# Four spill and four gather transfers per chunk in place of one and sixteen, and first-layer products done early in chunk 0

## What is computed

```python
dots = jnp.einsum('bfd,bgd->bfg', bottom_output, bottom_output)
pairs = dots[:, _TRIL_I, _TRIL_J]                     # 351 numbers per sample
x = jnp.concatenate([bottom_mlp_output, pairs, pad], axis=1)   # 480 wide
for w, b in ((w0, b0), (w1, b1), (w2, b2), (w3, b3)):  # 1024, 1024, 512, 256
    x = jax.nn.relu(x @ w.T + b)
return x @ w_out.T + b_out
```

## Time and profile before

| | us |
|---|---|
| median of 3 runs | 575.12 (574.05 to 575.9) |
| the profiled execution's own time | 574.64 |
| its span, first to last instruction | 572.8 |
| PE busy with matmuls | 90% of the span |
| ACT busy | 58% |
| POOL busy | 46% |
| DMA engines busy with SP's queue | 46% |

### The profile page before, as it was taken

How to read it: one execution, slowest core, us unless ns; L and a number is a source line. 1 busy time by engine, 2 the same in 40 slices (tenths; PEclk the granted TensorE clock), 3 DMA queues, 4 the chain that set the end, 5 groups by cost and what they waited for, 6 DMA issues and landing times.

```text
span 572.8 us, 13768 instructions
## 1 busy us (share of the span) xinstructions
PE 515.9 (90%) x4073; PEld 506.0 (88%) x4073; DVE 280.3 (49%) x646; ACT 334.4 (58%) x844; POOL 262.5 (46%) x467
## 2 busy tenths in 40 slices
PE   6948977999999699969999699979999699979997
PEld 6938976999999699969999699969999699979996
DVE  2845875527751477326761377316761377412111
ACT  3635799527982389525992389625993289613112
POOL 2801266224773177513773167613774167623321
PEclk9987999899999799998999799998999799997999
DMA  9978572255722576127732577117732477110000
GB/s 243 281 259 197 135 117 46 79 92 79 112 35 78 85 119 109 62 40 121 116 50 75 84 116 114 62 32 122 117 57 74 77 126 110 46 41 1 1 1 1
DMA packets 263088, 53.16 MB, mean 93 GB/s; under 512 B 248950, under 2 KB 260246, under 8 KB 263062
## 3 DMA queue, kind: packets, MB, share of 16 engines
q1 hardware_dynamic: 262374, 52.66, 46.0%
q10 hardware_dynamic: 688, 0.16, 0.1%
HBM read 45.71 MB, written 7.09 MB: 92 GB/s over the span
## 4 chain that ended last, share of the span: by engine, by line
PE 66%; SPq 11%; DMA 8%; ACT 4%; issue 4%; POOL 3%; DVE 2%; ACTq 1%; POOLq 0%
PE acc L684 52%; SPq L378 11%; PE gram_ps L647 8%; DMA blocks<-grams 5%; ACT parts L775 3%; PE gram_ps L630 3%; DMA pairs<-blocks 2%; PE gram_ps L601 2%; ACT h_full L791 1%; PE turned_ps L606 1%; ACTq L378 1%; POOL parts L526 1%; POOL grams L533 1%; DMA early_rows<-in_r_bottom_output_dram 1%; DVE grams L888 1%
## 5 line engine op out<-in xcount | busy, mean ns | idle before, releaser
L684 PE MATMUL acc<-h_a,w_hi 128*128 128x256 f32 x1152 | 216.0, 286 | 1.4 <-POOL h_a L541 1.2
L684 PEld LDWEIGHTS acc<-h_a,w_hi 128*128 128x128 f32 x1152 | 180.2, 193 | 3.3 <-POOL h_a L541 2.8
L791 ACT ACTIVATE h_full<-acc,small_t 128x256 f32<-128x256 f32 x176 | 82.6, 473 | 148.7 <-PE acc L684 146.2
L541 POOL TENSOR_TENSOR h_a<-h_full,h_a 128x256 fp32r<-128x256 f32 x96 | 72.3, 753 | 204.0 <-DVE h_a L908 204.0
L684 PE MATMUL acc<-h_a,w_lo 128*128 128x256 f32 x576 | 163.2, 283 | 0.0
L775 ACT ACTIVATE parts<-gram_ps 27x216 f32<-27x216 f32 x448 | 152.4, 340 | 16.0 <-PE gram_ps L647 6.5
L684 PE MATMUL acc<-x,w_hi 128*128 128x256 f32 x512 | 109.9, 313 | 34.3 <-ACT h_full L791 25.8
L684 PEld LDWEIGHTS acc<-x,w_hi 128*128 128x128 f32 x512 | 91.3, 219 | 36.1 <-issue 22.8
L684 PEld LDWEIGHTS acc<-h_a,w_lo 128*128 128x128 f32 x576 | 110.8, 192 | 0.0
L684 PE MATMUL acc<-h_b,w_hi 128*128 128x256 f32 x512 | 94.2, 285 | 2.4 <-POOL h_b L541 2.4
L908 DVE CAST h_a<-h_full 128x256 fp32r<-128x256 f32 x96 | 29.2, 304 | 123.3 <-ACT h_full L791 123.3
(11 more groups left out here) (49 smaller groups left out, 390.0 us busy)
## 6 DMA issues: line engine op xcount, KB each, us to landing
rows<-in_r_bottom_output_dram SPq DMA_DIRECT2D x444, 64.0 KB, 2.0
blocks<-grams SPq DMA_DIRECT2D x8, 864.0 KB, 3.5
w_raw<-in_L_rec_w_dram SPq DMA_DIRECT2D x6, 1024.0 KB, 7.5
early_rows<-in_r_bottom_output_dram SPq DMA_DIRECT2D x12, 224.0 KB, 6.0
stage_pairs<-in_L_rec_w_dram SPq DMA_DIRECT2D x1, 1408.0 KB, 9.5
w_raw<-in_L_rec_w_dram SPq DMA_DIRECT2D x2, 512.0 KB, 8.9
mlp_rows<-r_bottom_mlp_output_dram SPq DMA_DIRECT2D x8, 128.0 KB, 2.2
pairs<-blocks SPq DMA_DIRECT2D x32, 31.5 KB
```

What stands on the lines that cost most here:

```text
L541: nc.gpsimd.tensor_tensor(h[:, m, 1, :], h_full[:, slot % 2, :], h[:, m, 0, :].bitcast(F32), ALU.subtract).then_inc(split_done, 1)
L684: last = nc.tensor.matmul(acc_slot(slot), weight(wp, layer, m, k), in_tile(layer, k, xp), start=(k == 0 and n == 0), stop=(k == K_TILES[la ...
L791: nc.scalar.activation(h_full[:, slot % 2, :], acc_slot(slot), ACT.Relu, bias=small_t[:, slot:slot + 1]).then_inc(drained, 1)
```

## The change

`blocks` gets a new shape: for each of the 32 by 27 pairs of features now lie all 256 samples of the chunk together, 1 KB, the four quads' 64 behind one another.

- A gather piece is one transfer with runs of 1 KB; a chunk takes four gather transfers.
- A spill is four transfers, one for each quad (`spill_quad`). A quad's partition still reads its 6,912 bytes in one row, but they go to 27 places in DRAM, 256 bytes in each.
- In chunk 0, SP spills quads 0 and 1 and ACT quads 2 and 3. ACT does so before its copy of the bottom network's tile and of the weight groups.
- SP loads units 0 to 3 of chunk c+2 before the spill of chunk c+1, not after its gather.
- In chunk 0 the products of row tile 0 (k = 0) of the output tiles m = 0 to 5 come first, ahead of every product with pairs (`EARLY_TILES`). Tiles 2 and 3 are summed in the banks of `turned_ps`, tiles 4 and 5 in two banks of `gram_ps`. The weight groups 9 to 24 then have two banks, where they had four: PE waits at group n until DVE is done with group n - 2. The hooks still fire after every six matmuls, so groups 9, 10 and 11 are turned among the early products.

```diff
@@ -64,7 +64,7 @@
 EARLY_BY_ACT = 1
-OUT_HOOK = 2
+OUT_HOOK, EARLY_TILES = 2, 6
@@ -140,7 +140,7 @@
             steps.append(("early", u - XT_LAG))
-    steps.append(("mlp",))
+    steps += [("spill",), ("mlp",)]
     for n in range(BEFORE_CHUNK):
@@ -172,24 +172,30 @@
+    def products(layer, m, k, k1):
+        nonlocal done
+        while k < k1:
+            n = k1 - k
+            if layer < 2:
+                n = min(n, (every - done % every) // 3)
+            steps.append(("mm", layer, m, k, k + n))
+            k += n
+            done += 3 * n
+            if layer < 2 and done % every == 0 and hooks:
+                steps.extend(hooks.pop())
+            if done == OUT_HOOK * every:
+                steps.append(("out",))
+    if first:
+        for m in range(EARLY_TILES):
+            products(0, m, 0, 1)
     for layer in range(3):
...
                 steps.append(("mlp",))
-            k = 0
-            while k < K_TILES[layer]:
-                n = K_TILES[layer] - k
-                if layer < 2:
-                    n = min(n, (every - done % every) // 3)
-                steps.append(("mm", layer, m, k, k + n))
-                k += n
-                done += 3 * n
-                if layer < 2 and done % every == 0 and hooks:
-                    steps.extend(hooks.pop())
-                if done == OUT_HOOK * every:
-                    steps.append(("out",))
+            products(layer, m, 1 if first and layer == 0 and m < EARLY_TILES else 0, K_TILES[layer])
     if gram:
@@ -301,7 +307,7 @@
         y_view = y.rearrange("(c n) o -> c o n", n=CHUNK)
-        blocks = nc.dram_tensor("blocks", (GROUP, QUAD, FEATS, RUN), F32).ap()
+        blocks = nc.dram_tensor("blocks", (QUAD, FEATS, CHUNK), F32).ap()
@@ -311,7 +317,10 @@
-        def acc_slot(slot):
+        def acc_slot(c, slot):
+            if isinstance(c, int) and c == 0 and 2 <= slot < EARLY_TILES:
+                return (turned_ps if slot < 4 else gram_ps)[:, slot - 2, 0:CHUNK]
             return acc[:, slot % ACC_RING, 0:CHUNK]
@@ -328,7 +337,8 @@
-            return gram_ps[:, n % (GRAM_RING * GRAM_BANKS), :]
+            among = EARLY_TILES // 3 if BEFORE_CHUNK <= n < LATE_WEIGHTS else GRAM_RING * GRAM_BANKS
+            return gram_ps[:, n % among, :]
@@ -370,12 +380,14 @@
+        def spill_quad(engine, s):
+            engine.dma_start(blocks[:, :, s * RUN:(s + 1) * RUN], grams[QUAD * s:QUAD * (s + 1)]).then_inc(spilled, 16)
         def gather_piece(engine, f, nf, nk, q):
-            for s in range(GROUP):
-                src = bass.AP(blocks.tensor, (s * QUAD * FEATS + (FEATS + 1) * f + 1) * RUN,
-                              [[(FEATS + 1) * RUN, nf], [RUN, nk], [1, RUN]])
-                engine.dma_start(pairs[q % P:q % P + nf * nk, q // P, s * RUN:(s + 1) * RUN], src).then_inc(gathered[q // P], 16)
+            src = bass.AP(blocks.tensor, ((FEATS + 1) * f + 1) * CHUNK, [[(FEATS + 1) * CHUNK, nf], [CHUNK, nk], [1, CHUNK]])
+            engine.dma_start(pairs[q % P:q % P + nf * nk, q // P], src).then_inc(gathered[q // P], 16)
@@ -429,16 +441,17 @@
-            def spill(d):
+            def spill(d, quads=range(GROUP)):
...
                     sp.wait_ge(early_moved, UNITS)
-                sp.dma_start(blocks.rearrange("s f g r -> (s f) (g r)"), grams[:, :, :].rearrange("p g r -> p (g r)")).then_inc(spilled, 16)
+                for s in quads:
+                    spill_quad(sp, s)
             def gather(d, pieces=PIECES):
-                sp.wait_ge(spilled, (d + 1) * 16)
+                sp.wait_ge(spilled, (d + 1) * GROUP * 16)
                 if isinstance(d, int) and d == 0:
@@ -459,11 +472,11 @@
                         store_y(c - 1)
-                spill(c + 1)
-                gather(c + 1)
                 if not (isinstance(c, int) and c == CHUNKS - 2):
...
                         load_rows(c + 2, u)
+                spill(c + 1)
+                gather(c + 1)
@@ -483,7 +496,7 @@
                 load_weights(1, w1, 2 * i, 2 * i + 2, w1_loaded[i])
-            spill(0)
+            spill(0, (0, 1))
             load_weights(1, w1, 6, 8, w1_loaded[3])
@@ -529,7 +542,7 @@
-                    pool.wait_ge(spilled, d * 16)
+                    pool.wait_ge(spilled, d * GROUP * 16)
                 nc.gpsimd.tensor_tensor(
@@ -566,6 +579,9 @@
                     pe.wait_ge(grams_done, UNITS)
+                elif BEFORE_CHUNK <= n < LATE_WEIGHTS:
+                    pe.wait_ge(w_done, max(n - 1, BEFORE_CHUNK))
                 elif ring <= n < LATE_WEIGHTS:
@@ -666,10 +682,11 @@
-                        pe.wait_ge(w_done, groups_for(layer, m))
-                    if not (isinstance(c, int) and c == 0 and slot < ACC_RING):
-                        pe.wait_ge(drained, slot_count(c, slot) - ACC_RING)
+                        pe.wait_ge(w_done, W0_GROUPS if layer == 0 and m >= 4 else groups_for(layer, m))
+                    if not (isinstance(c, int) and c == 0 and slot < EARLY_TILES):
+                        of = slot - EARLY_TILES if isinstance(c, int) and c == 0 and slot < M_TILES[0] else slot - ACC_RING
+                        pe.wait_ge(drained, slot_count(c, of))
                 for k in range(k0, k1):
@@ -681,7 +698,7 @@
                     for n, (wp, xp) in enumerate(((w_hi, 0), (w_hi, 1), (w_lo, 0))):
-                        last = nc.tensor.matmul(acc_slot(slot), weight(wp, layer, m, k), in_tile(layer, k, xp),
+                        last = nc.tensor.matmul(acc_slot(c, slot), weight(wp, layer, m, k), in_tile(layer, k, xp),
                                                 start=(k == 0 and n == 0), stop=(k == K_TILES[layer] - 1 and n == 2))
@@ -788,7 +805,7 @@
                     act.wait_ge(weighed, 2 * c - 1 + slot)
-                nc.scalar.activation(h_full[:, slot % 2, :], acc_slot(slot), ACT.Relu,
+                nc.scalar.activation(h_full[:, slot % 2, :], acc_slot(c, slot), ACT.Relu,
                                      bias=small_t[:, slot:slot + 1]).then_inc(drained, 1)
@@ -797,7 +814,7 @@
                 for t in range(3):
-                    act.wait_ge(gathered[t], (d + 1) * 16 * GROUP * PIECES_OF[t])
+                    act.wait_ge(gathered[t], (d + 1) * 16 * PIECES_OF[t])
                     nc.scalar.activation(x0[:, 1 + t, 0, :], pairs[:, t, :], ACT.Copy).then_inc(pairs_hi_done, 1)
@@ -833,8 +850,13 @@
                     early_move(step[1])
+                elif step[0] == "spill":
+                    act.wait_ge(grams_done, UNITS)
+                    act.wait_ge(early_moved, UNITS)
+                    for s in (2, 3):
+                        spill_quad(nc.scalar, s)
                 elif step[0] == "gather":
-                    act.wait_ge(spilled, 16)
+                    act.wait_ge(spilled, GROUP * 16)
                     act.wait_ge(pairs_zeroed, 1)
```

## The result

The changed kernel takes 534.5 us (532.18 to 538.76, 4 runs); the kernel before took 574.89 in the same session. The ratio is 0.9305, with a 95% interval from 0.9243 to 0.9367: 7% faster, 40.4 us. I had said 533, with a range from 528 to 549. A second session gave 533.4 us and a ratio of 0.9293 (0.9262 to 0.9325).

The account below looks back on a forecast made before the run. The prediction took late pairs, held by one queue's 16 gather issues, to bound the kernel; the 572.8 us span less 38.2 (boundaries, last chunk's start) and 3.5 (chunk 0), plus 1.84 outside, gave 533 us, range 528 to 549.

Parts of the forecast that it names:

- The bound: Ends of chunks: PE's drain wait is ACT's wait for pairs; 11.8 of 17.0 us are one queue's issue time.
- Gather: Each boundary: four issues replace 16, so the gather takes 4.9 us, bounds 4.5 and 6.5.
- Spill: Each boundary: writing 3,456 pieces of 256 B takes 5.4 us, bounds 3.5 and 9.5.
- The disputed price: Spill: writing a 256 B piece costs the gather's 19 ns, 4.1 us in all; the skill's read-modify-write rule suggested double.
- the latency: Spill: 1.3 of the old spill's 3.5 us were not engine time, and were kept for the new spill.
- first rival: Spill: short writes cost double, spill 9.5 us, pairs 2.0 late; 548 us, 560 with the low clock; chance 0.18.
- Sum and slack: Boundaries: spill plus gather 10.3 us against a 12.4 us deadline, 2.1 to spare; chunks 58.6 us apart, saving 38.2.
- signs that I had set for being wrong: Profile: ACT still waiting for pairs at chunk ends, spill over 7.5 us, or PE gaps at chunk 0's weight groups.
- third rival: Spill: quad writes crawl; break-even 12.1 us, 50 ns a piece; at 65 ns, 600 us; chance 0.04.
- Chunk 0: Start: spill landed 38.1, tile 1 at 41.5, PE at weight group 11 at 44.5; gain 3.5 us, bounds 0 and 6.
- two banks in place of four: Chunk 0's weight groups: costs nothing; otherwise each of 14 groups would give back a few tenths.
- Reordered row loads: SP's queue: sixteen loads ahead of the spill, 8.5 us of issue, fit in its 13 us waits for the last sums.

Follow-up runs that it names:

- gather_16_issues: Changed kernel with each gather transfer cut back into four of 256 B runs, 16 issues a chunk: 595.18 us, ratio 1.0372.
- spill_written_twice: Changed kernel, but from chunk 1 on each quad's sums are also written to a second scratch, and the gather waits for all eight transfers: 571.22 us, ratio 0.9952.
- split_behind_groups: Changed kernel with ACT's and DVE's splits of chunk 0's pairs moved behind weight groups 9 to 11: 533.98 us, ratio 0.9303.
- chunk0_all_three: Changed kernel with chunk 0's pair splits behind weight groups 9-11, fourth w1 load behind SP's gather, ACT's gather issues behind group 7 and biases: 532.82 us.
- early_only: Kernel before with only the early products and two banks added; old spill, sixteen gather transfers and SP order: 573.78 us, ratio 1.0006.
- rows_behind_gather: Changed kernel with the sixteen row loads back behind the gather instead of ahead of the spill: 533.86 us, ratio 0.929.
- spill_two_queues: Changed kernel with ACT issuing quads 2 and 3 of every spill and SP quads 0 and 1: 535.38 us, ratio 0.9324.

## Why the prediction was right, point by point

**The bound.** PE's wait for a drain was a wait for pairs, and the pairs waited for issues. `gather_16_issues` shows it: with 16 issues the gap is there again, and larger.

**Gather, 4.9 us forecast.** 5.4 us measured (241.55 to 246.95). Four issues took 3.06 us, 0.77 each where I had 0.74, and from the last issue's start, 2.3 us in, to the landing there were 3.1 us instead of 2.65. My figure was a little too low, and the measured one lies inside the bounds of 4.5 and 6.5.

**Spill, 5.4 us forecast.** 6.68 measured, inside the bounds of 3.5 and 9.5. The disputed price was right: 19.4 ns a piece against the 19 that I took, and 4.3 us for a whole further copy against 4.1. The term that was too small is the latency, the 1.3 us left over by the old single transfer. With four transfers it is 2.35, of which 0.3 to 0.4 go away with a second queue. An issue took 0.86 us, not 0.53, though that too lies mostly beside the data. That the first rival's price didn't come can be said of the piece itself: writing 256 B takes the engine time of reading it, and 128 B take 12.2 ns where the row loads of that length had 13. The Trainium skill, "DMA: Bandwidth & Descriptors" (Specifications), has a read-modify-write below 512 B; no doubling of a piece shows in these rows.

**Sum and slack.** 10.3 us forecast, 12.1 measured; the deadline of 12.4 us was 12.5. Of 2.1 us to spare 0.43 were left. The forecast of 58.6 us a chunk held exactly, because the error of 1.8 us stayed below the slack, not because it was small. One of the signs that I had set for being wrong, that ACT still waits for pairs at the ends of chunks, is there in the letter: 0.48 us at the end of chunk 1. It comes from these two terms and reached PE nowhere. Three splits in one go, as I had it, are found at the end of chunk 0 only. The boundaries and the last chunk's start gave 38.4 us against 38.2.

**The first rival.** Its mechanism was refuted, and its size as well. I priced 4.1 us more on the spill at 548 us, or 560 with the clock, and 4 us of each were for chunk 0. `spill_written_twice` has 4.3 more, none of it in chunk 0, and takes 571: the lateness counts from a slack of 0.43 and not of 2.1 us, and the low clock does come behind each gap. So the boundaries cost 37 us where I had 11, or 24 with the clock. Had the pieces cost double, the range up to 549 would have missed far. The third rival's break-even moves down likewise, from a spill of 12.1 us to about 11.5 (`spill_written_twice`, with 11.0, is 3 us under the kernel before, half a microsecond a boundary).

**Chunk 0, 3.5 us forecast.** The spill was seen at 37.94 and 37.87, forecast 38.1. Then tile 1 came at 44.9 and 43.45, not at 41.5; more was left of the weight load than I took, or something else held it, and the runs don't part these. Group 11 followed at 48.63 and 46.75, not 44.5.

One step of this part of the prediction failed: two banks in place of four were to cost nothing, and PE was to go through its 18 matmuls at once. I had group 7 copied at 40.2 (measured 39.90) but not what hangs on it. With two banks group 9 waits for DVE to be done with everything up to group 8 (`max(n - 1, BEFORE_CHUNK)` in the change; the text there says group n - 2, which is not so for n = 9), and DVE was done at 41.28. With four banks group 5 would have been enough, and DVE was through group 6 at 37.99. So PE stood 3.35 and 3.19 us at group 9, and came to group 11 at 45.86 and 45.36, so that it could not have gone on at 44.5 even with the pairs at 41.5. There it stood another 2.77 and 1.40 us for group 9's subtraction, which was behind the pairs' splits. By the prediction's own words, gaps of PE at the weight groups of chunk 0 were to be a sign of being wrong; for chunk 0 they are. From group 12 to group 24 there is no wait for a bank in either profile. What the two gaps cost in the end is not known: `split_behind_groups` is free of the second and `chunk0_all_three` nearly free of both, and neither is clearly faster.

What the whole of chunk 0 gave must be told by times, 40.4 and 40.7 us in two sessions less the 38.4 of the boundaries: 2.0 and 2.3 us. That is made of two parts which I had not priced apart: the new layout alone gains 38.2 and 36.8 us over all, that is, it loses 0.2 and 1.6 in chunk 0, and the early products bring some 2.7. All these remainders carry the uncertainty of the 38.4, some 2 us. By `early_only` the early products bring nothing measurable in the old layout (its ±0.2% is 1.2 us), where group 9 waits for eight gather issues of ACT and not for two.

**Reordered row loads, no cost.** `rows_behind_gather`, 533.86 us: so it is.

**What came out right by luck.** The total of 533 against 534.5 and 533.4 hides a gather and a spill forecast 1.8 us too short, which the slack absorbed, and a chunk 0 forecast 1.2 to 1.5 us too good, by way of a PE that was to have no gap at group 9. That the slack was just large enough, with 0.43 us left, is luck as well.

## What to carry to other kernels

Where one queue issues many small transfers on the critical path and the DMA engines are mostly idle, count issues, not bytes: a layout in DRAM that makes the writer's pieces short can pay if it cuts the reader's issues to a quarter. Before relying on a slack, price both terms of what must fit in it with their fixed part, and measure what lies beyond the edge: here 4 us past it cost 37 of 40 us, half as much again as the lateness itself, because PE's granted clock is 0.50 behind each of these gaps. And where one stage's time varies by 7 us between executions of one program, read the rest of the run apart from it, and trust only medians for that stage.

## What the runs showed that I had not expected

- Chunk 0 of the same code ended at 122.8, 124.6, 125.7, 125.9 and 129.9 us in five executions (two of the changed kernel, one each of `spill_written_twice`, `rows_behind_gather` and `spill_two_queues`, which differ from it in SP's and ACT's issues near the end of chunk 0 alone), with a granted clock from 0.50 to 1.00 in the same window, 45 to 50 us.
- Pieces of 128 B cost the engines 12.2 ns, pieces of 256 B 19.4 ns: halving them raised the spill's engine time by a quarter only.
- A spill of four transfers has 2.35 us that do not grow with its data, against 1.3 for the same bytes in one transfer; two queues in place of one took off 0.3 to 0.4.
